# A fused attention and expert kernel: states in 64x64 blocks, their place in the quad, masks and transfers

## The chip, the cores and the metric

One core of a Trainium2 chip runs the kernel. The metric is the device time in microseconds (us), lower is better. Engines: TensorE (PE, with its weight loads PEld), VectorE (DVE), ScalarE (ACT), GpSimd (POOL) and SyncE (SP), which issues most DMAs. TensorE's clock has two levels, 1.2 and 2.4 GHz; the profile gives the granted clock as a share of the higher one.

## The reference, cut to what matters

```
xn = layernorm(x)                      # x: 8 x 1024 tokens of 128 values, float32
q, k, v = heads(xn @ W_qkv)            # 16 heads of 8 values
k = layernorm over each head's 8 values
for each chunk of 64 tokens:           # a scan; S is an 8x8 state for each head
    out = S @ q + (causal(q k^T)) v
    S = S + v^T k
attn = out @ W_o
e = argmax(xn @ centroids.T)           # one of 8 experts for each token
moe = a * (xn + w2[e] relu(w1[e] LN(xn) + b1[e]) + b2[e]) + (1 - a) * xn,  a = sigmoid(xn . centroid_e)
result = x + attn + moe
```

## The kernel before

The 8192 tokens are 64 tiles of 128. A **quad** is four tiles, one 128-token chunk position of four of the eight sequences; there are 16 quads (`n`), each walked in four steps (`i`), one tile (`m = 4n + i`) a step. Each engine has its own program, written out by hand in this order, and engines meet only through semaphores; an engine runs its program strictly in order, so whatever stands ahead of a waiting instruction's release delays it.

Each step on TensorE is `scores(m)` (16 matmuls of 32x64 blocks into the left halves of the four PSUM banks `SC[0..3]`), then `products(m-1)`. `scores(m)` may start only when VectorE's `score_mask(m-1)` has read the four banks (for m < 38 ScalarE and GpSimd take the first bank, VectorE three). Between the steps stand, for the quad itself, `inter_first`, `inter_second` (state times q) and `state_step` (the states' increments, 32 matmuls of 64x32 into banks FA and FB), and for the next quad `q_project`, `kT_project`, `k_transpose`, `v_project` and two `x_transpose` (from quad 7 on the experts' weights in their place), all through the same two banks FA and FB. ScalarE and VectorE empty these banks; VectorE also makes layer norm statistics, the running count that routes tokens (`choose`, `count`, `first_rows`, `places`), and `b1_fold` for each expert. Heads are 8 wide, so a state is kept as 32x32 blocks, of which `gmask` keeps the 8x8 diagonal blocks.

From quad 9, step 2 on, when `places` is done, GpSimd scatters the 64 tiles of normalised rows to the DRAM tensor `slots_d`, sorted by expert. SP writes zeros over `slots_d` first (8 DMAs from `zrow`, ahead of the expert weights and of the fourth and later token loads). After the scatters SP loads 71 slot tiles into the ring `xs`; before the first it issues `store_quad(14)`, which waits for `result(14)`. Then the expert stage runs: 71 times transpose, up, relu, down, and a scatter-add to the output.

TensorE's order within a quad before (n > 0):

```
i=0: scores, products, inter_first, state_step
i=1: scores, products, q_project, kT_project, output(n-1)
i=2: scores, products, k_transpose, wait qT_sb, x_transpose FA, inter_second, (odd n: affinities)
i=3: scores, products, x_transpose FB, v_project into FA, (odd n: affinities_back)
```

## Time and profile before

| | us |
|---|---|
| median of 3 runs | 438.86 |
| lowest and highest | 431.12, 442.11 |
| the profiled execution | 436.52 |
| its span (first to last instruction) | 434.5 |
| mean granted clock | 0.933 |

The profile is of one execution, whose time is 2.0 us more than its span. Attention and its tail take the span up to 280.9 us, the experts the rest. In the timelines, "idle before <- X" is the time that an engine sat waiting, and what released it; "issue" is a wait for nothing that the profile shows.

### The profile page before, as it was taken

The page shows a single profiled execution, that of the slowest core. Times are in us where ns is not written, and L with a number is a line of the kernel's source. Part 1 is how long each engine was busy: PE and PEld are TensorE (multiplying, and loading weights), DVE is VectorE, ACT ScalarE, POOL GpSimd, SP SyncE. Part 2 cuts the span into 40 slices and gives each one's busy share as a digit, 9 for nine tenths or more (in the row PEclk, how much of TensorE's full clock was granted, in tenths as well). Part 3 has the DMA queues.
Part 4 walks back from the last instruction along what each step waited for, and adds up shares of the span by engine and source line. Part 5 has one row for each costly group of instructions (what it writes and reads, how often), then busy time and mean ns, then how long its engine had stood idle before and what let it go on. Part 6 is the DMA issues. An engine that isn't in the chain of part 4 may idle for free.

```text
span 434.5 us, 19312 instructions
## 1 busy us (share of the span) xinstructions
PE 372.7 (86%) x7882; PEld 309.8 (71%) x7883; DVE 296.5 (68%) x780; ACT 228.2 (53%) x620; POOL 257.1 (59%) x270
## 2 busy tenths in 40 slices
PE   6767978878889799689779888799999999999992
PEld 6446656556567567467557566589999999999991
DVE  5655738667677477777675577738977867787770
ACT  3452625536446447726526436046676666766661
POOL 5153653544636232277777773008888788888885
PEclk9868969899899899969989899969999999999998
DMA  7996303123011011134344342304545455455540
GB/s 229 295 250 184 83 21 100 43 59 100 7 51 51 27 29 52 39 115 132 101 133 123 103 134 82 78 24 59 74 63 72 64 70 71 67 76 63 74 50 1
DMA packets 63079, 37.49 MB, mean 86 GB/s; under 512 B 5336, under 2 KB 60688, under 8 KB 62992
## 3 DMA queue, kind: packets, MB, share of 16 engines
q1 hardware_dynamic: 50720, 27.72, 24.2%
q0 software_dynamic: 12272, 8.54, 14.0%
q8 instruction: 63, 1.03, 1.0%
q14 instruction: 24, 0.20, 0.2%
HBM read 18.72 MB, written 17.97 MB: 84 GB/s over the span
## 4 chain that ended last, share of the span: by engine, by line
PE 42%; issue 26%; DVE 14%; POOL 12%; ACT 3%; DMA 1%; POOLq 1%; SPq 0%; DVEq 0%; ACTq 0%
POOL out_dram L418 12%; PE sc L1120 8%; PE bank L1170 6%; PE bank L1046 5%; PE bank L1054 4%; PE bank L1077 3%; PE bank L1179 3%; DVE pr L740 3%; ACT qx L461 2%; PE bank L1018 2%; PE bank L1154 1%; PE bank L1104 1%; DVE vp L725 1%; PE bank L1088 1%; PE sc L1009 1%
## 5 line engine op out<-in xcount | busy, mean ns | idle before, releaser
L418 POOL DMA_INDIRECT out_dram<-qx,xs x71 | 114.9, 1619 | 49.1 <-DVE qx L899 26.4
L600 ACT ACTIVATE qx<-sc,b1T 128x128 f32<-128x128 f32 x284 | 81.2, 368 | 47.2 <-PE sc L1265 47.1
L740 DVE TENSOR_TENSOR pr<-sc,causal 128x768 f32<-128x768 f32 (+1 forms) x64 | 67.8, 1060 | 16.9 <-PE sc L1120 16.2
L1265 PE MATMUL sc<-wide,ws 128*128 128x128 f32 x568 | 77.9, 281 | 0.0
L363 POOL DMA_INDIRECT slots_d<-rows,pos_i x64 | 63.2, 987 | 24.5 <-issue 24.5
L1273 PE MATMUL bank<-ws,qx 128*128 128x128 f32 x568 | 75.7, 277 | 0.4 <-ACT qx L600 0.4
L1265 PEld LDWEIGHTS sc<-wide,ws 128*128 128x128 f32 x568 | 70.7, 196 | 0.6 <-issue 0.2
L1273 PEld LDWEIGHTS bank<-ws,qx 128*128 128x128 f32 x568 | 69.7, 193 | 0.6 <-ACT qx L600 0.6
L1120 PE MATMUL sc<-qx,kT 32*64 32x128 f32 x2048 | 48.5, 291 | 22.0 <-DVE pr L740 17.3
L461 ACT ACTIVATE qx<-bank,gmask 128x512 f32<-128x512 f32 x64 | 41.3, 688 | 47.1 <-PE bank L1046 47.1
L354 POOL TENSOR_TENSOR pr<-pr,causal 128x256 f32<-128x256 f32 x38 | 27.6, 727 | 54.3 <-ACT pr L486 53.6
L1120 PEld LDWEIGHTS sc<-qx,kT 32*64 32x64 f32 x2048 | 31.8, 136 | 34.3 <-issue 30.3
L885 DVE COPY ws<-xT 128x1024 f32 x71 | 53.5, 754 | 0.9 <-issue 0.9
L1170 PE MATMUL bank<-pr,vz 128*32 128x64 f32 x2048 | 46.4, 232 | 3.0 <-issue 2.9
L1170 PEld LDWEIGHTS bank<-pr,vz 128*32 128x32 f32 x2048 | 34.7, 116 | 15.8 <-issue 15.6
L486 ACT ACTIVATE pr<-sc 128x256 f32<-128x256 f32 x38 | 14.6, 383 | 49.8 <-PE sc L1120 49.4
L879 DVE TENSOR_SCALAR wide<-xs 128x128 f32<-128x128 f32 x71 | 21.2, 301 | 27.7 <-DMA xs<-slots_d 27.1
L771 DVE TENSOR_TENSOR res<-bank,res 128x512 f32<-128x512 f32 x16 | 11.1, 691 | 37.0 <-PE bank L1179 37.0
L899 DVE SCALAR_TENSOR_TENSOR qx<-bank,xs,qx 128x128 f32<-128x128 f32 x71 | 24.5, 346 | 7.9 <-PE bank L1273 7.7
L594 ACT ACTIVATE wide<-sc 128x128 f32<-128x128 f32 x71 | 20.7, 293 | 13.9 <-PE sc L1258 13.9
L336 POOL TENSOR_SCALAR rows<-xin,mv,rstd 128x128 f32<-128x128 f32 x35 | 27.7, 801 | 0.0
L1046 PE MATMUL bank<-xT,wqkv 128*128 128x512 f32 x32 | 23.7, 832 | 2.1 <-ACT xT L448 1.5
(152 smaller groups left out, 537.5 us busy)
## 6 DMA issues: line engine op xcount, KB each, us to landing
xs<-slots_d SPq DMA_DIRECT2D x71, 66.0 KB, 2.1
slots_d<-zrow SPq DMA_DIRECT2D x7, 594.0 KB, 9.0
res<-in_L_attn_x_dram SPq DMA_DIRECT2D x16, 256.0 KB, 3.0
out_dram<-res SPq DMA_DIRECT2D x16, 256.0 KB
xin<-in_L_attn_x_dram SPq DMA_DIRECT2D x7, 512.0 KB, 4.3
w1raw<-in_L_ffn_w_dram SPq DMA_DIRECT2D x8, 256.0 KB, 4.3
w2raw<-in_L_ffn_w_dram SPq DMA_DIRECT2D x8, 256.0 KB, 5.8
out_dram<-qx,xs POOLq DMA_INDIRECT x71, 3.4
```

What stands on the lines that cost most here:

```text
L336: last = pool.tensor_scalar(rows[:, t, 0:D], xin[:, c % 2, b, :], mv[:, t, 0:1], rstd[:, t:t + 1], ALU.subtract, ALU.mult)
L363: pool.indirect_dma_start(slots_d, bass.IndirectOffsetOnAxis(ap=pos_i[:, t:t + 1], axis=0), rows[:, t, :], None, bounds_check=NS * P - 1, ...
L418: pool.indirect_dma_start(out_rows, bass.IndirectOffsetOnAxis(ap=xs[:, a, D + 2:D + 3].bitcast(U32), axis=0), ye[:, a, :], None, bounds_ch ...
L461: ins = nc.scalar.activation(qx[:, n % 2, :, j, :], FA[:, :].rearrange("p (i t) -> p i t", t=P), ACT.Copy, scale=gmask[:, j * DK:j * DK + 1])
L600: last = nc.scalar.activation(ht[:, k % 2, c * P:(c + 1) * P], SC[2 + k % 2][:, c * P:(c + 1) * P], ACT.Relu, bias=b1T[:, bass.ds(e * FC + ...
L740: nc.vector.tensor_tensor(pr[:, m % 2, a:G, :].rearrange("p g (j t) -> p g j t", t=CH), sc[:, a * BANK:G * BANK].rearrange("p (g j t) -> p ...
L885: nc.vector.tensor_copy(ws[:, k % 3, :], wts[:, bass.ds(e * WE, WE)]).then_inc(s("ws_ready"), 1)
L1046: mm(FA[:, :], wqkv[:, 0:D], xT[:, HALF * n:HALF * (n + 1), :].rearrange("p i t -> p (i t)"), start=True, stop=True).then_inc(s("q_ps"), 1)
L1120: last = mm(SC[g][CH * up:CH * (up + 1), c * PAIRS * CH:(c + 1) * PAIRS * CH], kT[r, n % 2, tok], qx[r, n % 2, i, 2 * up:2 * up + 2, CH * ...
L1170: last = mm(Y[half][SW * g:SW * (g + 1), i * P + CH * c:i * P + CH * (c + 1)], vz[:, half, c, i, g, p, :], pr[:, m % 2, g, k:k + CH], star ...
L1265: last = mm(SC[2 + k % 2][:, c * P:(c + 1) * P], ws[:, k % 3, c * P:(c + 1) * P], xsT[:, k % 2, :], start=True, stop=True)
L1273: last = mm(banks[k % 2][:, 0:D], ht[:, k % 2, c * P:(c + 1) * P], ws[:, k % 3, F + c * D:F + (c + 1) * D], start=(c == 0), stop=(c == FC ...
```

## The change

- States are kept as 64x64 blocks (`GW = 64`): `state`, `smid` and `dstate` are twice as wide, a new mask `smask` is made once, and `state_step`, `inter_first`, `inter_second` take half as many matmuls.
- `state_step(n)` writes the right halves of `SC[2]` and `SC[3]` and stands ahead of `scores(4n)` (in quad 0 ahead of `scores(1)`). VectorE's `dstate_mask(n)` is one instruction of 128x512 behind `score_mask(4n)`, and `scores(4n+1)` waits for it (`dst_sb`).
- The orders within the quad are new. TensorE's after:

```
i=0: state_step, scores, products, inter_first, kT_project
i=1: wait dst_sb, scores, products, k_transpose, q_project, output(n-1)
i=2: scores, products, v_project into FB, inter_second, (odd n: affinities)
i=3: scores, products, wait qT_sb, x_transpose FA, wait v_sb, x_transpose FB, (odd n: affinities_back)
```

- VectorE takes `score_mask` first in each step; `k_var` and `k_rstd` go to step 1, `v_scale` to step 2, `b1_fold(n-8)` from step 3 of quads 9 and on to step 1 of quads 8 and on. GpSimd takes `mask_scores` first and fills `vz` for the next quad in step 3.
- SP writes the zeros from `xs`, 8 slots for each partition's row, one DMA a quad in quads 0 to 8; `lbb`, `b2b` and the first expert weights are loaded in quads 2 to 5.

```diff
-        zrow = sb("zrow", [P, ROW])
+        GW = 64
+        state = sb("state", [P, B, GW])
+        smid = sb("smid", [P, HALF, GW])
+        dstate = sb("dstate", [P, NC, HALF, GW])
+        smask = sb("smask", [P, GW])
...
             def zero_slots(i):
-                last = min((i + 1) * ZERO, NS)
-                sp.dma_start(slots_v[:, i * ZERO:last, :], bcast(zrow[:, :], 1, last - i * ZERO))\
-                  .then_inc(s("slots_zero"), 16)
+                rows_of = slots_d.rearrange("(p k) r -> p k r", p=P)
+                last = min(RING * (i + 1), NS)
+                sp.dma_start(rows_of[:, RING * i:last, :], xs[:, 0:last - RING * i, :]).then_inc(s("slots_zero"), 16)
...
-            for i in range(NCH):
-                zero_slots(i)
-            for e in range(RAW):
-                load_expert(e)
...
                 if n:
                     store_quad(n - 1)
                     load_resid(n + 1)
+                if RING * n < NS:
+                    zero_slots(n)
+                if n == 2:
+                    sp.dma_start(lbb[:, :, :], ln_b.partition_broadcast(P)).then_inc(s("lb_in"), 16)
+                if n == 4:
+                    sp.dma_start(b2b[:, :, :], b2.partition_broadcast(P)).then_inc(s("b2_in"), 16)
+                if 3 <= n < 3 + RAW:
+                    load_expert(n - 3)
...
-            pool.memset(zrow[:, :], 0.0).then_inc(s("zrow_ready"), 1)
+            pool.memset(xs[:, :, :], 0.0).then_inc(s("zero_ready"), 1)
...
             def dstate_mask(n):
                 dve.wait_ge(s("ds_ps"), n + 1)
                 reach(dve, s("state_ready"), n)
-                nc.vector.tensor_tensor(dstate[:, 1, :, :], FB[:, 0:HALF * SW].rearrange("p (i k) -> p i k", k=SW),
-                                        bcast(gmask[:, :], 1, HALF), ALU.mult).then_inc(s("dsb_sb"), 1)
+                nc.vector.tensor_tensor(dstate[:, :, :, :], sc[:, 2 * BANK:4 * BANK].rearrange("p (c k) -> p c k", c=NC)
+                                        [:, :, BANK - HALF * GW:BANK].rearrange("p c (i k) -> p c i k", k=GW),
+                                        bcast(bcast(smask[:, :], 1, HALF), 1, NC), ALU.mult).then_inc(s("dst_sb"), 1)
...
             def state_step(n):
                 for i in range(HALF):
-                    for g in range(G):
-                        for c, bank in ((0, FA), (1, FB)):
-                            r, k = slice(CH * c, CH * (c + 1)), slice(i * D + SW * g, i * D + SW * (g + 1))
-                            last = mm(bank[SW * g:SW * (g + 1), i * SW:(i + 1) * SW], kn[r, n % 2, k], vp[r, k], start=True,
+                    for a in range(P // GW):
+                        for c in range(NC):
+                            r, k = slice(CH * c, CH * (c + 1)), slice(i * D + GW * a, i * D + GW * (a + 1))
+                            at = BANK - HALF * GW + i * GW
+                            last = mm(SC[2 + c][GW * a:GW * (a + 1), at:at + GW], kn[r, n % 2, k], vp[r, k], start=True,
                                       stop=True)
...
                 reach(pe, s("so_sb"), m)
+                if n or i > 1:
+                    pe.wait_ge(s("dst_sb"), n + (i > 0))
+                if i == (n == 0):
+                    state_step(n)
...
-                if n == 9 and i == 1:
-                    b1_fold(0)
-                if n >= 9 and i == 3:
+                if 8 <= n and i == 1:
                     b1_fold(n - 8)
```

## Rows read from the trace of the kernel before

**Rows 1.** The stages: us, then each engine busy (x instructions), granted clock, DMA.

```profile
15.25:53.75 38.50, 29.42 (x776) 20.79 (x780) 24.32 (x75) 17.98 (x38) 17.13 (x27) 0.82 0.81 190
53.75:183.75 130.00, 109.74 (x3259) 78.69 (x3259) 89.86 (x262) 68.11 (x137) 55.38 (x87) 0.93 0.17 48
183.75:280.88 97.13, 79.59 (x2549) 60.50 (x2549) 68.40 (x114) 41.34 (x76) 63.16 (x64) 0.93 0.37 112
```

**Rows 2.** Waits of TensorE in 40 to 280: total us, times, longest.

```profile
PE sc L1120 <- DVE pr L740: 17.3, 13, 2.8
PE bank L1104 <- issue: 9.5, 5, 3.2
PE bank L1170 <- issue: 2.9, 3, 1.5
PE bank L1018 <- ACT qT L469: 2.6, 6, 0.4
```

**Rows 3.** Timeline of TensorE: start, us; a quad with little waiting.

```profile
127.28 0.65 PE L1143 MATMUL bank<-qT,state 32*32 32x64 f32 x32 [0.76 <-issue]
127.85 0.76 PE L1104 MATMUL bank<-vp,kn 64*32 64x32 f32 x64
128.54 0.69 PE L1120 MATMUL sc<-qx,kT 32*64 32x128 f32 x32
...
129.75 1.13 PE L1046 MATMUL bank<-xT,wqkv 128*128 128x512 f32 x2
...
139.91 0.72 PE L1143 MATMUL bank<-qT,state 32*32 32x64 f32 x32
```

**Rows 4.** The same: quad 2 with a gap, and the start of quad 9.

```profile
55.10 0.65 PE L1143 MATMUL bank<-qT,state 32*32 32x64 f32 x32 [0.22 <-issue]
...
58.67 1.11 PE L1120 MATMUL sc<-qx,kT 32*64 32x128 f32 x18 [1.84 <-issue]
...
60.72 2.08 PE L1046 MATMUL bank<-xT,wqkv 128*128 128x512 f32 x2
...
172.82 0.65 PE L1143 MATMUL bank<-qT,state 32*32 32x64 f32 x32
```

**Rows 5.** Timeline of all engines where a quad meets the next.

```profile
142.14 0.23 DVE L826 TENSOR_TENSOR total<-total 128x128 bf16<-128x128 bf16 x1
...
143.38 0.77 PE L1120 MATMUL sc<-qx,kT 32*64 32x128 f32 x32 [2.06 <-DVE pr L740]
```

**Rows 6.** Instruction groups by shape: busy us, mean ns, idle before.

```profile
L740 DVE TENSOR_TENSOR pr<-sc,causal 128x768 f32<-128x768 f32 x38 | 36.1, 949 | 13.2 <-PE sc L1120 13.0
...
L740 DVE TENSOR_TENSOR pr<-sc,causal 128x1024 f32<-128x1024 f32 x26 | 31.8, 1222 | 3.7 <-PE sc L1120 3.2
...
L725 DVE TENSOR_TENSOR vp<-bank,krs 128x512 f32<-128x512 f32 x16 | 11.1, 691 | 9.3 <-PE bank L1077 9.1
...
L777 DVE TENSOR_TENSOR w1raw<-w1raw,lbb 128x512 f32<-128x512 f32 x8 | 5.5, 690 | 0.2
...
L326 POOL MEMSET vz<- 128x1024 f32 x4 | 3.6, 942 | 0.0
```

**Rows 7.** DMA queues of the page: packets, MB, share of 16 engines.

```profile
q8 instruction: 63, 1.03, 1.0%
```

**Rows 8.** Timeline of TensorE in the first quad.

```profile
26.38 0.88 PE L1104 MATMUL bank<-vp,kn 64*32 64x32 f32 x64 [4.07 <-ACT qT L469]
```

**Rows 9.** Timeline of GpSimd: the first and the last of 64 scatters.

```profile
183.75 1.22 POOL L363 DMA_INDIRECT slots_d<-rows,pos_i  x1 [5.26 <-issue]
...
265.13 0.97 POOL L363 DMA_INDIRECT slots_d<-rows,pos_i  x1 [0.30 <-issue]
```

**Rows 10.** Timeline of all engines where the experts begin.

```profile
274.76 0.38 SPq L267 DMA_DIRECT2D out_dram<-res  x1
...
275.25 5.41 SPq L284 DMA_DIRECT2D xs<-slots_d  x8
...
280.88 0.66 PE L1258 MATMUL sc<-ident,wide 128*128 128x128 f32 x2 [1.70 <-DVE pr L740]
```

More of the change, by code:

```diff
@@ L402, in _ @@
                         ln_norm(n + 2, (4,))
+                if i == 3 and n + 1 < LATE:
+                    values_own(n + 1)
                 if m >= ROUTED:
@@ L690, in _ @@
             dve.wait_ge(s("pool_m"), 7)
+            nc.vector.tensor_reduce(out=smask[:, :], in_=headmask[:, :].rearrange("p (g k) -> p k g", k=GW), axis=AX,
+                                    op=ALU.add)
             nc.vector.tensor_reduce(out=gmask[:, :], in_=headmask[:, :].rearrange("p (g k) -> p k g", g=G), axis=AX,
@@ L914, in _ @@
                 stat = n + 2 < NCH
-                if i == 1 and n:
-                    dstate_mask(n)
                 score_mask(m)
                 if i == 0:
+                    if n:
+                        dstate_mask(n)
+                    if n >= LATE:
+                        state_steps(n)
                     if n == 0:
@@ L921, in _ @@
                         ln_moments(2)
+                    if norm:
+                        ln_inverse(n + 2)
+                        ln_norm(n + 2, (5, 6, 7))
                     if n == 8:
@@ L928, in _ @@
                 if i == 1:
-                    if n >= LATE:
-                        state_steps(n)
-                    if norm:
-                        ln_inverse(n + 2)
-                        ln_norm(n + 2, (5, 6, 7))
-                    if n == 0:
-                        dstate_mask(n)
+                    if n == 0:
+                        dstate_mask(0)
+                    if stat:
+                        ln_stats(n + 3, range(4))
+                    if more:
+                        k_var(n + 1)
                     if n:
                         result(n - 1)
-                    if stat:
-                        ln_stats(n + 3, range(4))
                     if n in (2, 4, 6):
@@ L946, in _ @@
                         places()
+                    if more:
+                        k_rstd(n + 1)
                 if i == 2:
+                    if more:
+                        v_scale(n + 1, FB)
                     if stat:
                         ln_stats(n + 3, range(4, B))
-                    if more:
-                        k_var(n + 1)
                     if n == 8:
@@ L955, in _ @@
                     if more:
-                        k_rstd(n + 1)
-                        v_scale(n + 1, FA)
                         values_across(n + 1)
@@ L1037, in affinities_back, with first_left, second_left @@
                 last.then_inc(s("aff_ps"), 1)
+            def first_left(n):
+                pe.wait_ge(s("xT_sb") if n + 1 < NCH else s("w1_sb"), 2 * n + 3 if n + 1 < NCH else n - 6)
+            def second_left(n):
+                pe.wait_ge(s("xT_sb") if n + 1 < NCH else s("w2_sb"), 2 * n + 4 if n + 1 < NCH else n - 6)
             def q_project(n):
@@ L1140, in inter_first @@
                     for i in range(HALF):
-                        for g in range(G):
-                            r = slice(SW * g, SW * (g + 1))
+                        for a in range(P // GW):
+                            r = slice(GW * a, GW * (a + 1))
                             last = mm(Y[half][r, i * P:i * P + CH], state[r, half * HALF + i, :],
@@ L1151, in inter_second @@
                 for i in range(HALF):
-                    for g in range(G):
-                        r = slice(SW * g, SW * (g + 1))
+                    for a in range(P // GW):
+                        r = slice(GW * a, GW * (a + 1))
                         last = mm(Y[half][r, i * P + CH:(i + 1) * P], smid[r, i, :], qT[r, half, i * P + CH:(i + 1) * P],
@@ L1206, in _ @@
                     inter_first(n)
-                    if n:
-                        state_step(n)
-                    else:
-                        q_project(1)
-                        kT_project(1)
+                    if more:
+                        kT_project(n + 1)
                 if i == 1:
-                    if n == 0:
-                        state_step(0)
-                    elif more:
+                    if more:
+                        k_transpose(n + 1)
                         q_project(n + 1)
-                        kT_project(n + 1)
                     if n:
@@ L1221, in _ @@
                     if more:
[L1222 to L1229 removed]
+                        v_project(n + 1, FB)
                     inter_second(n)
@@ L1239, in _ @@
                     if more:
-                        pe.wait_ge(s("kn_sb"), n + 2)
+                        pe.wait_ge(s("qT_sb"), n + 2)
+                    if norm:
+                        x_transpose(2 * n + 2, FA)
+                    elif n - 7 < E:
+                        w1_transpose(n - 7)
+                    if more:
+                        pe.wait_ge(s("v_sb"), n + 2)
                     if norm:
@@ L1244, in _ @@
                         w2_transpose(n - 7)
-                    if more:
-                        v_project(n + 1, FA)
                     if n < 8 and n % 2 == 1:
```

101 lines of the change are left out of this document (32 added, 69 removed).

## Prediction

> **What bounds the kernel now.** I read the stages first [rows 1]. Between 15 and 281 us TensorE is busy for four fifths of the time and no other engine comes near that, so its order and its waits set the attention's pace; behind 281 us the experts run on code that the change doesn't touch, and I take their 153.6 us (434.5 less 280.9) over unchanged. Next, the quads. Quad 2 begins its `inter_first` at 55.10 and quad 9 at 172.82 [rows 4]: seven quads in 117.7 us, 16.8 each. The quad that waits least, from 127.28 to 139.91 [rows 3], takes 12.6, and 0.4 of that is the wait for `qT_sb` (2.6 us in six times [rows 2]). Odd quads up to 7 add the affinities, two instructions for each column block over 512 columns and four transposes: an estimate of 1.5 us, from the 1.13 that the q projection's two take [rows 3]. So work alone makes 12.2 to 13.7 us a quad, about 12.9 on the average, and some 4 us a quad are something else.
>
> The list of waits tells what [rows 2]. TensorE's scores wait for VectorE's mask 13 times, 17.3 us; batches of small matmuls stop in the middle, 9.5 us in `state_step` (L1104) and 2.9 in the products (L1170), with nothing in the profile that releases them. The rest is the clock: after the 1.84 us gap at 58.67 the same q projection takes 2.08 us [rows 4] against 1.13 [rows 3]. That is the lower of the two levels, and it shows in the granted 0.93 and 0.82 of the stages [rows 1]. A gap of 2 us costs about 2 us again.
>
> The mask waits have a pattern: at 142.14 VectorE ends the running count, only then takes the mask of the next quad's first scores, and TensorE has waited 2.06 us by 143.38 [rows 5]. The b1 fold stands in the same place from quad 9 on.
>
> At the end there is a second chain. The 64 scatters start at 183.75 and the last starts at 265.13, 1.29 us apart on the average [rows 9], whatever TensorE does. SP then waits for `result(14)`, stores it at 274.76, loads the slots from 275.25, and the experts' first transpose runs at 280.88 [rows 10]. So the scatters have some 6 us of slack, the end of `places` is 97.1 us ahead of the experts, and a faster attention behind quad 9 can give no more than the slack.
>
> **64x64 blocks.** `state_step` goes from 64 to 32 instructions and each `inter` from 32 to 16. Start to start, the state step takes 0.69 us (127.85 to 128.54) and the inter 0.57 (127.28 to 127.85) [rows 3]. If the count of instructions sets this, half of each goes: 0.35 and twice 0.28, 0.9 us a quad. If each block of the array works through its own list, nothing goes: a block of the inter has 8 instructions of 64 columns before and after, and the state step's 8 for each block go from 32 to 64 columns, as the inter's have now, and weight loads are twice as wide; that would be worse by up to 0.5 us a quad. The state step issues 64 in 0.69 us where the inter issues 32 in 0.57, so time doesn't go by the count alone, and not by columns alone either (half the columns, more time). I take a gain of 0.3 us a quad, near the middle, 5 us over 16 quads.
>
> The Trainium skill (TensorEngine Tiling (Array Packing), Instruction Overhead) says that a small matmul costs the same up to about 60 columns. By that rule the wider, fewer instructions would be nearly free and the gain the 0.9 us; the two rates just named speak for only part of it. The sum doesn't use the rule.
>
> **The gaps inside batches.** The page has a queue for instructions, 63 packets and 1.03 MB, 16 KB each [rows 7]. Five of the eight gaps [rows 2] lie in `state_step`, the densest stretch: state step, scores and products of 128 matmuls and their loads in about 1.9 us. I read them as instructions that come late. The change thins this: the state step stands ahead of the first scores, has half the instructions, and the kT projection (1 us, two matmuls) follows the inter. TensorE has some 2,000 instructions fewer, of over 15,000. I expect about 3 of the 12.4 us to stay, and with the clock that follows, a gain of some 14 us, nine of it ahead of quad 9's scatters.
>
> The Trainium skill (Runtime: NRT & Kernel Launch, Instruction fetch mechanics) has instructions fetched in 16 KiB blocks, which is the packet size of the row, and calls the cost of crossing a block mostly hidden. If it is hidden here, the gaps have another cause; rival two has this.
>
> **The new wait.** `scores(4n+1)` now waits for `dstate_mask(n)` behind `score_mask(4n)`: 0.95 us for three banks or 1.22 for four, and 0.69, the 128x512 read of a bank at L725 [rows 6], the nearest row; with two hops of about 0.1, 1.9 or 2.1 us after the scores. TensorE has products 0.6, inter 0.3 to 0.6 and kT 0.9 to 1.0 between them, 1.8 to 2.2. Cover is just there, 0 to 0.3 us short; but where VectorE comes late to the first mask, all of the lateness now shows, where before some 0.7 us of it was hidden. Behind the wait stand scores, products and all later steps; GpSimd's state steps stand behind the same mask, with slack. The increments' PSUM columns weren't in use, so FA and FB are free earlier: the 0.4 us wait for `qT_sb` goes, since step 3 comes 3 us behind the copy.
>
> **VectorE's new order.** VectorE is busy 89.9 us in 130.0 [rows 1], 11.6 for each 16.8 us quad, routing included; the wider increments add 0.1 to 0.2. That is 0.5 less than TensorE's 12.2, so a quad without count or fold can meet every mask. The count of quads 2, 4 and 6 still stands behind step 3, and the 2 us wait of rows 5 stays, three times; in step 1 `choose` now meets `k_var`, which waits for ScalarE's square, and I allow 1.2 us in the same quads. The b1 fold is twice 0.69 [rows 6] and a small one, 1.55 us. In step 1 of a late quad VectorE has mask 1.22, 1.1 idle until the square (kT transpose, copy and square take 2.4 us behind the scores), `k_var`, `result` and `k_rstd` 2.0, fold 1.55, next mask 1.22: 7.2 us to `scores(4n+3)`. TensorE comes there with products, transpose, q, output, scores, products, v and inter, 5.7 us. So 1.5 us of wait in quads 10 to 15, where before the fold made the boundary wait as long: no gain and no loss. In quads 8 and 9 it meets count and places, some 3.7 us each. Sum: 6 + 4 + 9 in the quads up to 9 and later as before: 17.3 us of mask waits become some 17 to 22; with the count's and the fold's other places I book 2 us of loss ahead of the scatters. `places` ends 9.5 us into quad 9 against 11 before, which I book as 1.5 of gain.
>
> **Start and transfers.** GpSimd clears `xs` (1056 columns, by L326's 0.94 us for 1024 [rows 6]) ahead of the identity, in place of a small row: TensorE's warm-up starts 0.7 us later, and with it everything. In quad 0 the state step no longer waits for the next quad's expansions, 4.07 us [rows 8]. New is a wait of `k_transpose(1)` for ScalarE, whose `ln_root(2)` waits for VectorE's statistics, about 2 us. With the state step's place and the zeros out of the way of the token loads, I take 6 us of the 38.5 of quads 0 and 1 [rows 1]; bounds 2 and 9. The zeros (4.8 MB) in nine parts end with quad 8, ahead of the scatters; each goes behind the residual's load, whose data is due a quad later. The weights of the first experts are due in quad 7 and loaded in quads 3 to 5: no cost.
>
> **The sum.** Start +0.7. Quads 0 and 1: -6. From 53.75 to the scatters, 130.0 us [rows 1]: blocks -2.5, gaps with their clock -9, `qT_sb` -3, mask waits +2, `places` -1.5, clock from the shorter waits -1: -15, 115 left. From the first scatter to the experts, 97.1 us: scatters 81.4 + 1.3, landing 2.5, load and scale 4.5 as from 275.25 to 279.7, about 91: -6, if the quads keep pace, which at 6.6 quads of 13.7 they just do. Together -26.3: 436.5 becomes 410. The median before is 2.3 above the profiled execution, so 412.
>
> **The rivals.** *One, the forecast*, 412 (402 to 421): chance 0.55.
>
> *Two, the gaps stay*: their cause is DMA latency and the zeros, now a burst in every quad, meet the instruction packets. For it: the gaps were longest, 3.2 us, with scatters under way. Then 9 us come back ahead of the scatters, and the later quads take 15 us, which is longer than the scatters: 6 more. 427. Chance 0.2.
>
> *Three, VectorE becomes the bound*: with everything in step 1, `k_var` waiting for the square and `result` for the output hold the next mask in each quad, 1.5 us, and half of these drop the clock. 14 quads by 1.3 more than I take: 18 us, 430 to 434, no change to speak of. Chance 0.13.
>
> *Four, slower*: the mask and increment mask in line, at the quad's start, make TensorE wait 1.3 us in each quad with a second wait in step 1, and the clock stays low for the 4 us behind (2 us more), as after 58.67. At 3.3 us a quad it is 46 us over 14 quads, less the 26: 459. It decides where the added loss passes 1.9 us a quad. Against it: the 0.5 us that VectorE has to spare. Chance 0.07.
>
> *Five, more than forecast*: 64x64 at the full 0.9 us and the clock at its high level throughout. The end of `places` comes 12 us earlier, the scatters' 91 us stay: 400. Chance 0.05.
>
> Faster by over 2% (about what a measurement of this kernel can tell from no change) is under 430: one, two and five, 0.80, less 0.03 as two lies near the bound, 0.77. Within 2%: 0.16, three and that. Slower: 0.07. A range from 400 to 430 leaves out three and four, 0.2.
>
> **What would show it.** Right: scatters start at about 163 and the experts at 254, 91 us on; L1104's instructions halve and their gaps vanish; waits of the scores on VectorE sit in step 3 and at the end of even quads, some 20 us in all; the clock of 50 to 160 is above 0.95. Wrong: gaps inside batches with other lines, an increment mask over 0.8 us, 64x64 batches longer than 0.69, or experts that begin over 95 us after the first scatter.

## The result and the profile after

The changed kernel takes 417.0 us (median of 4 runs, 411.6 to 420.7), the kernel before 438.3 (431.1 to 442.1) beside it: a ratio of 0.955, 95% interval 0.946 to 0.964. It is faster, 5 us above the forecast's 412 and inside its range. All ratios here are taken over the fast executions of the two kernels, so they are not the quotients of the medians beside them. The profiled execution is the fastest of the four: 411.6 us, span 409.8; its partner of before is 436.5, span 434.5.

I read the same views in the same order as before. First the stages, cut at the first `inter` of quad 2 [rows 4] (the first cut of [rows 1] lies 1.35 us ahead of it), the first scatter and the experts' first transpose.

```profile
core 0: us, PE busy (x) PEld busy (x) DVE busy (x) ACT busy (x) POOL busy (x), PEclk, DMA share, GB/s
15.25:50.94 35.69, 27.02 (x740) 19.35 (x740) 28.42 (x85) 19.09 (x40) 18.36 (x28) 0.95 0.19 55
50.94:165.30 114.36, 102.49 (x2694) 75.29 (x2687) 96.77 (x248) 68.98 (x136) 59.94 (x85) 0.99 0.36 114
165.30:256.59 91.29, 75.01 (x2161) 57.05 (x2161) 69.26 (x106) 40.48 (x75) 63.71 (x64) 0.98 0.40 120
```

Quad 2's `inter` starts at 50.94, where it was 55.10 [rows 4]: -4.2. From there to the first scatter 114.4 us in place of 128.7 [rows 4, 9]: -14.3. From the first scatter to the experts 91.3 in place of 97.1 [rows 9, 10]: -5.8. The experts' own part, 153.2, is what it was (153.6). The three differences are 24.3 of the 24.7 us that the profiled executions differ by, and the granted clock of the middle stage is 0.99.

Next TensorE's waits from 40 to 265 us, against [rows 2] (scores are L1115 now, `state_step` L1094, products L1165, `inter_first` L1138):

```profile
engine line waited for: us in total, times, longest us
PE sc L1115 <- issue: 16.1, 14, 3.5
PE sc L1115 <- DVE pr L738: 3.0, 1, 3.0
PE bank L1138 <- issue: 2.5, 2, 1.3
PE sc L1115 <- DVE dstate L749: 2.2, 3, 0.9
PE sc L1246 <- DVE pr L738: 1.9, 1, 1.9
PE bank L1165 <- issue: 1.4, 3, 0.9
```

The waits for `qT` are gone, and so are the 9.5 us inside `state_step`. The waits for the mask are mostly among those of "issue" now: in ten of these 14 the mask ended 0.1 us ahead of the scores, though the view names no engine. Counted so, the scores wait for VectorE's masks 11 times, 17.3 us, and 2.2 us in three times for the increments' mask: 19.5 in all, against 17.3 before.

TensorE's time from its first scores to the experts is 25.0 us shorter, and it starts 0.7 later. Of the 25.0, 11.2 are idle time (47.7 us before, 36.5 after) and the rest is busy time, 218.8 before and 204.5 after. The two projections of 512 columns, whose work is unchanged, show most of it (two rows of before, two of after):

```profile
L1046 PE MATMUL bank<-xT,wqkv 128*128 128x512 f32 x32 | 23.7, 832 | 2.1 <-ACT xT L448 1.5 <-DVE dstate L750 0.5
L1054 PE MATMUL bank<-xT,wqkv 128*128 128x512 f32 x32 | 20.9, 742 | 1.4 <-issue 1.4
...
L1058 PE MATMUL bank<-xT,wqkv 128*128 128x512 f32 x32 | 17.9, 643 | 3.0 <-ACT xT L449 3.0
L1049 PE MATMUL bank<-xT,wqkv 128*128 128x512 f32 x32 | 16.4, 593 | 0.0
```

This is the clock. Each stage's busy time, multiplied by what its granted clock lacks to 1, adds up to 18.6 us before (0.82, 0.93, 0.93 [rows 1]) and 3.9 after (0.95, 0.99, 0.98): an estimate of 14.7 us, where the busy time fell by 14.2. The timeline of a late quad shows both kinds at once:

```profile
start us, us, engine line op out<-in xcount [idle before <-releaser]
185.09 0.69 PE L1094 MATMUL sc<-vp,kn 64*64 64x64 f32 x32 [0.17 <-issue]
185.72 0.69 PE L1115 MATMUL sc<-qx,kT 32*64 32x128 f32 x31
187.00 0.32 PE L1115 MATMUL sc<-qx,kT 32*64 32x128 f32 x1 [0.59 <-issue]
187.25 0.65 PE L1165 MATMUL bank<-pr,vz 128*32 128x64 f32 x32
187.83 0.68 PE L1138 MATMUL bank<-qT,state 64*64 64x64 f32 x16
188.44 1.13 PE L1058 MATMUL bank<-xT,wqkv 128*128 128x512 f32 x2
...
197.14 0.70 PE L1115 MATMUL sc<-qx,kT 32*64 32x128 f32 x32 [1.12 <-issue]
...
200.87 0.54 PE L1165 MATMUL bank<-pr,vz 128*32 128x64 f32 x23
202.31 0.35 PE L1165 MATMUL bank<-pr,vz 128*32 128x64 f32 x9 [0.91 <-issue]
```

At 197.14 the wait stands ahead of a whole batch, in step 3: VectorE's mask of the tile before, behind the b1 fold, runs from 195.81 to 197.03. At 187.00 and 202.31 it stands inside a batch that had all it needs, after 31 and after 23 of its 32 matmuls: a gap. Read off the timeline in this way from 16 us to the experts (a row of the same line as the row ahead of it, idle over 0.15 us, no engine named), the gaps are 11 with 16.2 us in the kernel before and 10 with 7.4 after. Start to start, the state step takes 0.63 us (185.09 to 185.72; 0.69 before [rows 3]) and the inter 0.61 (187.83 to 188.44; 0.57 before).

At the end of the quads, GpSimd's scatters and SP's queue, as in [rows 9, 10]:

```profile
165.30 1.22 POOL L365 DMA_INDIRECT slots_d<-rows,pos_i  x1 [5.91 <-issue]
...
247.24 0.97 POOL L365 DMA_INDIRECT slots_d<-rows,pos_i  x1 [0.30 <-issue]
```

```profile
250.62 0.38 SPq L261 DMA_DIRECT2D out_dram<-res  x1
251.10 4.02 SPq L286 DMA_DIRECT2D xs<-slots_d  x8
```

The load of the slots still follows the store of `result(14)`, so the quads and not the scatters end last, but the last scatter was issued only 3.9 us ahead of the load; before, it was 10.1.

### The profile page after: what moved, and what is told of

The parts are those of the page before. It is cut to its first block, busy times and chain, and to the rows that moved or that the text cites. A ratio compares the mean times of both kernels' runs of the same rounds, so it can differ in the third digit from the quotient of the medians.

```text
span 409.8 us, 17322 instructions
## 1 busy us (share of the span) xinstructions
PE 356.2 (87%) x6891; PEld 298.5 (73%) x6891; DVE 306.6 (75%) x765; ACT 228.9 (56%) x620; POOL 263.2 (64%) x270
## 4 chain that ended last, share of the span: by engine, by line
PE 43%; issue 24%; POOL 12%; DVE 10%; DMA 7%; ACT 2%; DVEq 1%; POOLq 1%; ACTq 0%
POOL out_dram L419 10%; PE sc L1115 9%; PE bank L1165 8%; DMA out_dram<-qx,xs 3%; DMA xs<-slots_d 3%; PE bank L1058 3%; PE bank L1071 3%; PE bank L1174 3%; PE bank L1049 3%; PE sc L1094 2%; PE bank L1064 2%; DVE pr L738 2%; PE bank L1138 2%; PE bank L1149 2%; PE bank L1077 1%
## 5 line engine op out<-in xcount | busy, mean ns | idle before, releaser
L596 ACT ACTIVATE qx<-sc,b1T 128x128 f32<-128x128 f32 x284 | 81.4, 368 | 47.4 <-PE sc L1253 47.4
L1253 PE MATMUL sc<-wide,ws 128*128 128x128 f32 x568 | 76.7, 278 | 0.0
L1253 PEld LDWEIGHTS sc<-wide,ws 128*128 128x128 f32 x568 | 69.7, 193 | 0.8 <-issue 0.2
L1115 PE MATMUL sc<-qx,kT 32*64 32x128 f32 x2048 | 47.4, 285 | 25.3 <-issue 17.8
L1115 PEld LDWEIGHTS sc<-qx,kT 32*64 32x64 f32 x2048 | 31.0, 133 | 45.9 <-issue 43.1
L1165 PE MATMUL bank<-pr,vz 128*32 128x64 f32 x2048 | 44.5, 227 | 3.5 <-POOL pr L356 2.0
L1165 PEld LDWEIGHTS bank<-pr,vz 128*32 128x32 f32 x2048 | 33.2, 112 | 15.6 <-issue 13.3
L338 POOL TENSOR_SCALAR rows<-xin,mv,rstd 128x128 f32<-128x128 f32 x35 | 27.7, 808 | 0.0
L888 DVE SCALAR_TENSOR_TENSOR qx<-b2b,xs 128x128 f32<-128x128 f32 x71 | 24.7, 347 | 0.1
L1246 PE MATMUL sc<-ident,wide 128*128 128x128 f32 x71 | 19.9, 283 | 5.3 <-DVE wide L876 3.3
```

The source lines that it names most:

```text
L338: last = pool.tensor_scalar(rows[:, t, 0:D], xin[:, c % 2, b, :], mv[:, t, 0:1], rstd[:, t:t + 1], ALU.subtract, ALU.mult)
L596: last = nc.scalar.activation(ht[:, k % 2, c * P:(c + 1) * P], SC[2 + k % 2][:, c * P:(c + 1) * P], ACT.Relu, bias=b1T[:, bass.ds(e * FC + ...
L1115: last = mm(SC[g][CH * up:CH * (up + 1), c * PAIRS * CH:(c + 1) * PAIRS * CH], kT[r, n % 2, tok], qx[r, n % 2, i, 2 * up:2 * up + 2, CH * ...
L1165: last = mm(Y[half][SW * g:SW * (g + 1), i * P + CH * c:i * P + CH * (c + 1)], vz[:, half, c, i, g, p, :], pr[:, m % 2, g, k:k + CH], star ...
L1253: last = mm(SC[2 + k % 2][:, c * P:(c + 1) * P], ws[:, k % 3, c * P:(c + 1) * P], xsT[:, k % 2, :], start=True, stop=True)
```

## The experiments

All ratios are to the kernel before, run beside it on the same chip. Each expectation stands as it was written before its run.

**1. The blocks alone.** The kernel before with 64x64 blocks, in its old banks and its old order.

```diff
-                    for g in range(G):
-                        for c, bank in ((0, FA), (1, FB)):
-                            r, k = slice(CH * c, CH * (c + 1)), slice(i * D + SW * g, i * D + SW * (g + 1))
+                    for g in range(P // GW):
+                        for c, bank in ((0, FA), (1, FB)):
+                            r, k = slice(CH * c, CH * (c + 1)), slice(i * D + GW * g, i * D + GW * (g + 1))
```

> The kernel before with the 64x64 blocks alone (increments still in FA and FB, the old order, masks and transfers as before). If a block of the array works through its own list, the state step stays near 0.65 us start to start and the two inter batches near 0.6, so the blocks give nothing by themselves; TensorE issues some 2,000 instructions fewer, so the gaps inside batches (12.4 us between 40 and 280 before) may fall to 7 or 8: time 0.98 to 1.0 of before, scatters start between 178 and 184 us. If the count of instructions sets the cost, each quad is 0.9 us shorter and the time is 0.96.

Measured: 425.4 us beside 434.6, ratio 0.982 [0.969, 0.996]. The gaps inside batches fell to 2 with 2.1 us. What took their place is in the list of waits:

```profile
PE sc L1124 <- DVE pr L744: 27.7, 18, 2.8
PE bank L1108 <- ACT qT L471: 4.9, 1, 4.9
PE bank L1147 <- issue: 2.5, 4, 0.8
```

TensorE, rid of the gaps, runs into VectorE's masks: from 40 us on these waits are 25.7 us in 16 times, against 17.3 in 13 [rows 2]. So its idle time hardly changes, and what the profiled execution gains (span 420.0) is mostly busy time, 206.8 us ahead of the experts in place of 218.8, at a mean clock of 0.954 in place of 0.933.

**2. The order alone.** The changed kernel with state step and inters in 32x32 blocks again.

```diff
-                    for a in range(P // GW):
+                    W = GW if n == 0 else SW
+                    for a in range(P // W):
...
```

> The changed kernel with the state step (from quad 1 on) and the inter batches in 32-wide matmuls again, same place, same increment mask. If gaps are instructions that come late, the denser stretch brings them back: gaps inside batches rise from about 6 us to 10 or more, time 0.965 to 0.975 of before, against 0.955 for the change. If the blocks matter neither for TensorE's work nor for the gaps, it stays at 0.955 within 0.003.

Measured: 439.5 us beside 434.6, ratio 1.023 [1.012, 1.034]. My number was wrong by five to six per cent. The waits:

```profile
PE sc L1116 <- issue: 18.2, 13, 3.4
PE bank L1166 <- issue: 8.7, 7, 3.7
PE bank L1139 <- issue: 5.4, 3, 2.9
```

There are 13 gaps with 17.6 us, in products and inters as well, and the scores' waits for masks are no fewer than before. From 15 us to the experts, in us (the masks with the increments'):

| | before | blocks alone | order alone | both |
|---|---|---|---|---|
| gaps inside batches | 16.2 | 2.1 | 17.6 | 7.4 |
| scores wait for masks | 17.3 | 27.7 | 17.6 | 20.7 |
| all idle time of TensorE | 47.7 | 46.7 | 46.1 | 36.5 |

So the two halves do different things. The blocks take 10 to 14 us of gaps away in either order. In the old order 10.4 us of that come back as waits for masks, in the new one 3.1. The order by itself takes away only the waits for `qT` (3.5 us from 40 us on); its worth is that it lets the blocks' gain through.

**3. The transfers.** The changed kernel with the zeros, biases and first expert weights at the start, as before.

```diff
...
+            for i in range((NS + RING - 1) // RING):
+                zero_slots(i)
+            for e in range(RAW):
+                load_expert(e)
```

> The changed kernel with all zeros, the two broadcast loads and the first three expert weights issued in the start again, ahead of the fourth token load. If the transfers' place was worth something, it shows in quads 0 and 1: the first inter batch of quad 2 starts 2 to 4 us later than 50.9. If it was worth nothing the same batch starts at 50 to 52 us and the time stays at 0.955.

Measured: 414.3 us, ratio 0.959 [0.948, 0.970]; quad 2 at 50.99, first scatter at 164.51, experts at 256.42. Each of the three within 0.8 us of the changed kernel, with 7 gaps of 6.4 us: spreading the transfers is worth nothing here.

**4. The b1 fold in step 3** of the late quads, where nothing on TensorE is close behind it.

```diff
-                if 8 <= n and i == 1:
+                if 8 <= n and i == 3 and m != NT - 1:
                     b1_fold(n - 8)
+                if m == NT - 2:
+                    b1_fold(E - 1)
```

> The changed kernel with the b1 fold at the end of step 3 (quads 8 to 14; the last in step 2 of quad 15). In the changed kernel VectorE idles 1.8 us ahead of the first mask of each late quad, so a fold of 1.55 us there should be hidden, and the 1.1 us waits ahead of the last scores of quads 10 to 14 and some 1.5 us of the waits in quads 8 and 9 should go. The scatters start 2 to 3 us earlier (near 163) and the experts as much, because the scatters' 81.4 us and what follows them stay: time 0.949 of before. If my count of VectorE's room is wrong, a wait of 1 to 1.5 us comes back at the end of each late quad and the time is 0.955 or above.

Measured: 413.9 us, ratio 0.958 [0.947, 0.970]. That is no better than the changed kernel, and not the 0.949 expected; only the profiled execution, 405.9, is much shorter. The first scatter went at 166.25, 0.95 later and not the 2 to 3 us earlier that I expected. The rows of that one execution still show what bounds the end. The 1.1 us waits of step 3 in the late quads are gone, and with them the end of the quads has another bound:

```profile
243.53 0.38 SPq L261 DMA_DIRECT2D out_dram<-res  x1
249.76 3.67 SPq L286 DMA_DIRECT2D xs<-slots_d  x8
```

```profile
253.68 0.66 PE L1248 MATMUL sc<-ident,wide 128*128 128x128 f32 x2 [7.16 <-DVE pr L738]
```

The store is 7.1 us earlier than in the changed kernel, the load only 1.3: it waits for the last scatter (issued at 247.40). TensorE stands 7.16 us ahead of the experts.

**5 and 6. How much cover the scatters have**, after and before: the first one held until the scores of tile 40 are done.

```diff
                     pool.wait_ge(s("gate_ready"), 1)
+                    pool.wait_ge(s("sc_ps"), 41)
```

> The changed kernel with the first scatter held until the scores of tile 40 are done (about 172.7 in place of 165.3, so 7.4 us later; the 64 scatters themselves, 82 us, are unchanged). Nothing else waits for them but the loads of the sorted rows. Theory: in the changed kernel the last scatter lands at 249.6 and the SP queue's first load of sorted rows starts at 251.1 behind the last stores, so there is about 1.5 us of cover and the experts' first transpose comes 5.5 to 6.5 us later, at 262 to 263; ratio to before 0.968. Rival (the scatters are as well covered as they were before): less than 2 us later.

> The kernel before with the first scatter held until the scores of tile 40 are done (about 191.2 in place of 183.75, 7.4 us later). Theory: before, the last scatter landed at about 267.5 and the first load of sorted rows started at 275.25, so 7.7 us of cover take up the whole delay and the experts' first transpose stays at 281, ratio 0.995 to 1.005. Rival: the scatters held the end of the quads already before; 5 to 7 us later, ratio 1.015.

Measured on the changed kernel: 421.6 us, ratio 0.974 [0.967, 0.980]. The first scatter went at 175.99 (10.7 later, more than planned), the store at 253.08, the load at 259.91:

```profile
253.08 0.38 SPq L261 DMA_DIRECT2D out_dram<-res  x1
259.91 3.67 SPq L286 DMA_DIRECT2D xs<-slots_d  x8
```

8.8 of the 10.7 us arrive at the load: 1.9 us of cover. Measured on the kernel before: 438.1 us, ratio 1.011 [1.004, 1.018]; the first scatter went at 188.06, 4.3 later and not the 7.4 meant, so the run does not try all of the cover. The load still follows the store:

```profile
276.57 0.38 SPq L267 DMA_DIRECT2D out_dram<-res  x1
277.06 5.01 SPq L284 DMA_DIRECT2D xs<-slots_d  x8
```

The last scatter was issued at 270.03 and lands 2.4 us on if it does as in experiment 4, so 4.6 us of cover were left of it. The ratio is 1 per cent above 1 all the same; the profile puts 1.8 us of that ahead of the store, in the quads, and why is open. The forecast's reading stands: the change ate the scatters' slack, 7.7 us before by the last scatter's issue and 2.4 of landing, down to 1.5 by the same sum and 1.9 by experiment 5.

**7. Places a step earlier.** `first_rows` moves to step 3 of quad 8, `places` to step 0 of quad 9.

```diff
                     if n == 9:
-                        first_rows()
+                        places()
...
                         tiles_rounded()
+                        first_rows()
```

> The changed kernel with first_rows in step 3 of quad 8 and places in step 0 of quad 9, everything else as changed. Theory: the scatters start about 4 us earlier (161 in place of 165.3), but here the late quads with the fold in step 1 are as late as the scatters, so the experts' first transpose stays at 255 to 256.6 and the time at 415 to 417, ratio 0.95 to 0.955. Rival (the scatters alone set the end of the quads): experts at 252.5, 413 us.

Measured: 415.7 us, ratio 0.960 [0.951, 0.969]; first scatter at 162.62, experts at 257.30. No gain, as the theory had it: with the fold in step 1 the quads end no earlier, and the load, at 251.82, follows the store of `result(14)` with the scatters long done (the last was issued at 244.68).

**8. Both together**, and the clearing of `xs` behind the identity.

```diff
+                if 8 < n and i == 3 and m != NT - 1:
+                    b1_fold(n - 8)
+                if n == 9 and i == 1:
+                    b1_fold(0)
...
-            pool.memset(xs[:, :, :], 0.0).then_inc(s("zero_ready"), 1)
             pool.wait_ge(s("pool_c"), 4)
```

> The changed kernel with what the runs so far point to: the b1 fold in step 3 (in step 2 of the last quad, that of expert 0 in step 1 of quad 9), first_rows in step 3 of quad 8 and places in step 0 of quad 9, so that the first scatter can start a step earlier, and the xs memset on GpSimd behind the ident select. My theory: with the fold in step 3 the end of the quads is set by the 64 scatters, which GpSimd issues one after the other in 81 us, so a first scatter at about 161 in place of 166.3 brings the experts' first transpose from 253.7 to about 249, less another 0.7 us from the start; 408 to 410 us beside a before of 438, ratio 0.935. First rival: the scores and products of quads 10 to 15 end no earlier than with the late fold, and the scatters' head start is lost; experts at 253, ratio 0.95. Second rival: the first_rows in step 3 of quad 8 (2.9 us, in place of the fold's 1.6) only move the wait; experts above 254.

Measured: 407.5 us (405.2 to 409.6, six runs), ratio 0.939 [0.934, 0.945], the best of all. First scatter 162.09, last one issued at 243.86, experts at 252.15. The chain of work that ended last still runs over the scatters:

```profile
243.86 4.37 DMA slots_d<-rows,pos_i
...
248.30 0.34 SPq L286
...
248.68 1.92 DMA xs<-slots_d
...
250.83 1.23 DVE pr L738
...
252.15 0.66 PE sc L1249 x2
```

The scatters' head start of 4.2 us over experiment 4 brought 1.5 at the load, since the last scatter took 4.37 us to land, not 2.4; this I had not expected and did not pursue.

**9. The last tile ahead of the first experts**: its mask, products, y, output and result ahead of the scaling and transposing of the first sorted rows.

```diff
-            se_trans(0)
-            se_trans(1)
             products(NT - 1)
-            se_up(0)
             output(NQ - 1)
+            se_trans(0)
+            se_trans(1)
+            se_up(0)
```

> The last best (fold in step 3, places a step earlier, memset later) and at the end of the quads: the last tile's mask ahead of the last fold, its products, y, output and result ahead of the first expert tiles' transposes, on all three engines. In the last best TensorE stood 6.59 us there, VectorE's last mask (1.22 us) sat behind the loads of the sorted rows, and the products and the output (1.0 and 1.06 us) lay between the first experts' matmuls. Theory: all of that fits into the wait for the scatters, so the experts' first transpose follows se_scale directly, 1.2 us earlier, and the products and output behind it are gone as well; 2 to 3 us less, 404.5 to 405.5 beside a before of 435, ratio 0.93. Rival: the result, now ahead of se_scale on VectorE, comes later than the sorted rows (the y copy and the output are a chain of three engines), and the gain is under 1 us.

Measured: 412.1 us (411.6 to 415.0), ratio 0.950 [0.945, 0.955]: 4.6 us slower than experiment 8. From the end of the last scores to the experts it is shorter, 6.4 us against 7.2, but the quads end 5 us later. The stage 200 to 245 has the same TensorE order in both kernels; first experiment 8, then this one:

```profile
200.00:245.00 45.00, 40.37 (x1198) 31.09 (x1189) 35.65 (x53) 22.12 (x41) 34.17 (x36) 1.00 0.39 120
```

```profile
200.00:245.00 45.00, 40.27 (x1072) 30.19 (x1061) 32.47 (x49) 22.12 (x41) 34.29 (x35) 0.92 0.38 114
```

In quad 13 a gap in the inter is 2.57 us here and 2.01 there, and the granted clock is lower behind it here. The state step of quad 13 begins at 207.91 here and 207.80 there, that of quad 14 at 226.03 and 222.60, that of quad 15 at 239.61 and 236.01. So 3.6 of the 4.2 us by which the experts begin later here are lost ahead of the first instruction that was moved, which is in step 2 of quad 15. Then I tried the mask's move alone.

```diff
                 if m == NT - 2:
+                    score_mask(NT - 1)
                     b1_fold(E - 1)
```

> The best so far with one line's move from the last experiment alone: VectorE's mask of the last tile ahead of the last fold instead of behind the scaling of the first sorted rows; the products, the output and the result stay where the changed kernel has them, so TensorE's, ScalarE's and GpSimd's orders are those of the best. Theory (the last experiment lost 5 us to a longer break in TensorE's supply in quad 13 and the lower clock behind it, 0.92 in place of 1.00 from 200 to 245, which has nothing to do with what was moved): where the scatters end last, the experts' first transpose comes 1.2 us earlier than in the best, and the time is 405 to 408, or, if the break and the clock fall as in the last one, 410 to 412 with the quads as late as there. Rival (the moves themselves cost the 5 us): 405 to 408 here, with the gap in quad 13 short. A time of 410 and more therefore speaks for the first, 406 leaves both.

It gave 490.5 us beside a before of 517.4, ratio 0.950 [0.943, 0.956]. Both kernels are some 80 us slower on that chip. In this one's trace TensorE's matmuls come in ever smaller groups from 162 us on and then one by one, one each 2.8 us at worst, until 252 us. That is the stretch in which the 64 scatters run, from 161.66 to 243.30; why is open. So neither its time nor its ratio can be set beside the others. In the profiled pair it was the gap in quad 13 and the clock behind it that cost experiment 9 most of its time, and not the moves; why all six of its executions are the slower ones stays open.

**10. What a gap is: its place.** 64 more transposes in the warm-up, 128 instructions with their weight loads.

```diff
-            keep_busy(12)
+            keep_busy(12 + 64)
```

> The changed kernel with 64 more transposes of the identity in the warm-up ahead of the first real transpose: 128 more TensorE instructions (each matmul has its weight load), while TensorE waits for the input anyway. Theory (a batch of matmuls is cut where TensorE's next piece of code isn't there yet, and a piece is 768 instructions, 376 matmuls with their loads and some 16 waits): every cut of the late quads comes 64 matmuls earlier in the program. In the changed kernel they fell in the scores batch after 31 of 32 matmuls (187.00), in the products batch after 23 of 32 (202.31), in inter_first after 15 of 16 (218.24), in the scores after 20 of 32 (233.91). 64 earlier, of 31 of the scores: the scores and products alternate in batches of 32, so the cut should lie one scores batch earlier at the same place, or in the projections between; in no case at the old places. Time, within the noise, as the changed kernel's 412 to 417 us. Rival (the cuts come from DMA traffic or from contention at a time): they stay near 187, 202, 218 and 234 us or at the same matmuls of the same step.

Measured (one run): 418.4 us. The gaps moved, and all by one amount:

```profile
193.24 0.45 PE L1115 MATMUL sc<-qx,kT 32*64 32x128 f32 x11
194.20 0.66 PE L1115 MATMUL sc<-qx,kT 32*64 32x128 f32 x21 [0.51 <-issue]
...
208.41 0.30 PE L1165 MATMUL bank<-pr,vz 128*32 128x64 f32 x2
210.30 0.65 PE L1165 MATMUL bank<-pr,vz 128*32 128x64 f32 x30 [1.59 <-issue]
```

In quad 11 the cut went from scores(44) after 31 to scores(45) after 11; with one matmul of the batch, the products, the inter and kT between them that is 1 + 32 + 16 + 2 + 11 = 62 matmuls later. In quads 12 and 13 it is 61 and 62 later, in quad 14 62 earlier. A grid of 128 matmuls with their loads, 256 instructions, moved by 64 does just this (the odd two would be the waits on semaphores in between, if they count as instructions, which no run shows). In contrast, experiment 5, whose scatters were 10.7 us late, has its gaps at the same matmuls as the changed kernel (after 31, 23, 15 and 20 at 189.63, 205.31, 220.66 and 236.57). The changed kernel and experiments 3, 4, 5, 7, 8 and 9, all seven, stop in the inter of quad 13 after 15 of 16, between 211.57 and 220.66 us. Traffic or a point in time is ruled out as what places the gaps; how long each is, 0.35 to 2.57 us at that one place, is not explained by this. My expectation had the grid at 768 instructions, three times too wide; in the changed kernel's late quads only every third line of the grid shows a gap, 375 or 376 matmuls apart, and why the third is open.

**11. What a gap is: its rate.** 1536 calls of the old state step's shape in one batch, ahead of everything. Each f32 call is two matmuls and two loads in the trace, so it is 6144 instructions, not the 3072 that I wrote, and 37 us of work.

```diff
+            for u in range(1536):
+                g, c = u // NC % G, u % NC
+                mm(SC[2 + c][SW * g:SW * (g + 1), 0:SW], ident[CH * c:CH * (c + 1), 0:SW],
+                   ident[CH * c:CH * (c + 1), 0:SW], start=True, stop=True)
```

> The changed kernel with 1536 small matmuls of the old state step's shape (64x32 by 64x32, a weight load each, 3072 instructions) in one batch ahead of the warm-up, where no scatter runs and nothing else is on TensorE. In the kernel before 64 of them took 0.69 us. If nothing but TensorE's own work bounds them, the batch takes 16.6 us without a break. Theory (the supply of instructions bounds dense stretches): breaks at regular distances of about 256 or 768 instructions, and a batch of 30 to 60 us, since the late quads of the changed kernel went through 768 instructions in 14.4 to 15.9 us and showed short breaks at that pace. The batch gives the sustained rate directly. The kernel as a whole is later by what the batch outlasts the input loads, some 15 to 45 us. Rival (the breaks come from traffic of the scatters and weights): 16.6 us, no break.

```profile
7.42 2.04 PE L1184 MATMUL sc<-ident 64*32 64x32 f32 x202
11.71 1.53 PE L1184 MATMUL sc<-ident 64*32 64x32 f32 x128 [2.26 <-issue]
16.81 1.54 PE L1184 MATMUL sc<-ident 64*32 64x32 f32 x128 [3.56 <-issue]
20.82 1.54 PE L1184 MATMUL sc<-ident 64*32 64x32 f32 x128 [2.47 <-issue]
24.27 1.54 PE L1184 MATMUL sc<-ident 64*32 64x32 f32 x128 [1.91 <-issue]
...
94.01 0.80 PE L1184 MATMUL sc<-ident 64*32 64x32 f32 x54 [2.46 <-issue]
```

Measured (one run): 514.2 us; the batch took 87.4. It runs 128 matmuls in 1.54 us and then stands still for 1.9 to 3.6, each time. The DMA queue for instructions has 24 packets more here than in the changed kernel (55), for 24 times 256 instructions: one packet of 16 KB is one step of the grid.

```profile
q8 instruction: 79, 1.29, 1.1%
```

From 20.82 to 94.01 there are 20 steps, 3.66 us each. So in this batch TensorE is fed 256 instructions in 3.66 us, about 70 a us, where it works them off in 1.54. No scatter runs at that time.

## Why the forecast was right, and where it was not

**The three stages** came out as summed: quads 0 and 1 with the start -4.2 against -5.3, then -14.3 against -15, then -5.8 against -6 (91.3 us from the first scatter to the experts, forecast 91). The mechanism is the forecast's, fewer stops and a higher clock; that each stage's sum fits so well is in part luck, since terms that were off cancel.

- In all, the forecast booked some 6 us for the clock (the 14 of the gaps less their own 9.4, and 1 more), and 5 for the blocks. The clock gave some 14 and the blocks nothing.
- Quads 0 and 1: the 4.07 us wait went, the new wait for `k_transpose(1)` did not come, but three others did (1.55, 0.96 and 1.97 us, for masks of VectorE and GpSimd). Idle time fell by 1.8 us only, busy time by 3.2.
- From there to the scatters: gaps -3.0, `qT` -3.1, three stops ahead of the inters -1.8, masks -0.4 (booked +2), busy time -6.5. `places` gave 1.1 (9.8 us into quad 9; booked 1.5).
- The last stage: the terms of the sum, 81.4, 1.3, 2.5 and 4.5, make 89.7 and not 91. The 1.3 that the sum lacks is about the last tile's mask, which stands between the scaling and the transpose (1.23 us in the chain of experiment 8). And it was the quads that ended last, by 1.5 us: the load waited for the store.

That the scatters' slack caps this stage was right as a bound: rows 9 and 10 showed it, and in experiments 4, 5 and 8 the load waits for the last scatter. The change came within 1.5 to 1.9 us of the cap without meeting it.

**64x64 blocks.** Forecast: 0.3 us less work a quad, between -0.5 and +0.9. By the start-to-start times they give 0.06 in the state step and cost 0.04 in each inter: nothing. The Trainium skill (TensorEngine Tiling (Array Packing), Instruction Overhead) says that a matmul of 1 column takes as long as one of 60; the prediction took half the time for half the instructions from it. The rows agree with that rule only block by block: in the state step each block of the array has 8 instructions before and after, of 32 columns in 0.69 us and of 64 in 0.63. So the rival reading in the prediction, each block's own list, was the right one, without the loss that it allowed for the wider columns. And the term was put in the wrong account. The blocks' worth is in the supply: without them the order gives nothing (experiment 2). Rival five, 400 us, needed the full 0.9 us a quad and is out for the same reason.

**The gaps.** Cause right (instructions that come late), size off: 12.4 us were to become 3, and by the measure above 16.2 became 7.4, 8.8 less where I had booked 9.4. They did not vanish but left `state_step` for whichever batch stands at the grid's line; gaps inside batches with other lines were one of the prediction's own signs of being wrong. The stretch inter, state step, scores, products was 160 matmuls, 320 instructions, in 2.47 us [rows 3]; fed at experiment 11's rate it would take 4.6, so it runs 2.1 us ahead of its supply. After, state step, scores, products and inter are 112 matmuls, 224 instructions, in about 2.4 us, and would take 3.2: 0.8. This is worked out, not shown. Where the Trainium skill (Runtime: NRT & Kernel Launch, Instruction fetch mechanics) calls the cost of a block's crossing mostly hidden, this case has 3.2 us for one in the kernel before [rows 2] and up to 3.56 in experiment 11; the measurement decides. Rival two, the zeros' bursts as cause of the gaps, is refuted by experiments 3 and 10. That other traffic makes a gap longer is not: the longest of the kernel before (2.23 and 3.24 us) fall among the scatters, and on the one chip of the run behind experiment 9 TensorE crawled for as long as they ran.

**VectorE.** In all the scores wait 19.5 us for masks, where the forecast had some 20. (Its parts as listed, 2 us three times, 1.2 three times, 3.7 twice and 1.5 six times, make 26, which it did not say.) The count's wait at the quads' boundary, forecast to stay at 2 us three times, shrank: it shows in step 1 as 0.93 us at 67.03 and 0.43 at 97.10, where the scores wait for the increments' mask, and not at all in the third quad. The waits behind `choose` are 0.96, 1.43 and 0.94 (forecast 1.2), and those of step 3 in the late quads are there as well: 3.0 and 3.5 us in quads 8 and 9 (forecast 3.7), 1.12 to 1.27 in quads 10 to 14 (forecast 1.5). "No gain and no loss" was too kind to them: experiment 4 shows that without them the scatters would have been the bound. Rival three took the same waits for larger than they are; rival four needed 1.9 us of loss in each quad.

**Transfers and start.** Spreading the zeros cost nothing, as forecast, but it gave nothing either (experiment 3), where the forecast had the zeros out of the token loads' way among the causes of its 6 us in quads 0 and 1. The warm-up starts at 2.68 in place of 1.95, 0.7 as costed.

**The median** lies 5.4 us above the profiled execution, where I had added 2.3; that is 3.1 of the 5 us between 417 and 412, and the rest is that execution itself, 411.6 where the sum gave 410.

## What to carry to other kernels

A gap inside a batch of small matmuls, released by nothing, was here a matter of how many instructions the dense stretch has, not of how long they run: count them against the rate at which they were fed (256 in 3.66 us in experiment 11), and halve the count where the array's work stays the same. What such stops cost is more than their own time: of 25 us gained, some 14 were the clock by the estimate above. Two limits that lie side by side, here the feed and VectorE's masks, hide each other: either edit alone gave 0.98 and 1.02, both 0.955. So a half that gives nothing alone is not yet worthless. And a serial chain beside the main one (64 scatters, 1.3 us apart) takes over as soon as its slack is gone; move its start together with the end of the other, as in experiment 8 (0.939).

## What was not expected of the hardware

TensorE's instructions came in 16 KB packets of 256, at 3.45 to 4.0 us each under full draw, 5.10 at the start (11.71 to 16.81), and a batch of the small shape uses one up in 1.54. The place of the stops is fixed in the program: the same matmul, kernel after kernel, until 128 instructions ahead of it moved them all by half a packet. The 64x64 blocks took nearly as long with half the instructions as the 32x32 and 64x32 ones with all. The last scatter took 2.4 us to land in one kernel and 4.37 in another.
